# First router of a Macaron block: transposed logits in four column groups, row copies moved behind the PSUM copies, and a quarter of the one-hot tiles on GpSimd

## The chip, the cores and the metric

The kernel runs on one core of one Trainium2 chip. The metric is the device time of one execution in microseconds. Before the change three runs gave a median of 1010.13 us (1009.66 to 1010.32).

## The reference, cut to what matters

The block is a mixture-of-experts feed-forward layer at half weight, attention, and the same feed-forward layer again; each has a layer norm in front. The change lies in the first feed-forward layer's router. There are 4 x 1024 tokens of 128 features, 8 experts with a capacity of 1280 slots each, and two experts per token.

```python
xt = x.reshape(n, D)                      # after the layer norm
logits = xt @ gate_w                      # n x 8
top_logits, top_idx = jax.lax.top_k(logits, k)
router_probs = softmax over the two chosen
exp_rank = cumsum(one_hot(top_idx)) - 1   # place of each token in its expert, first choices ahead
exp_mask = exp_mask * (exp_rank < cap)
exp_batches = einsum('nec,nd->ecd', sec_mask, xt)   # the rows of each expert
...
x = x + 0.5 * _L0_ffn_ref(_layernorm(x), ...)
```

## The kernel before, in words

The work runs in three stages, one code block per engine in each: the first feed-forward layer (from about 0 to 250 us), attention with the second router woven into it, and the second feed-forward layer. The engines' instruction streams are written out by hand and meet through semaphores; within an engine the order of the code is the order of execution. There is no planner.

The change touches only the first part of the first stage, the router. Its work, with the lines of the profile:

- **SyncE (SP)** loads x in four batches of 1024 tokens into `xin` (L758), loads the first two experts' weights (L764 to L766), stores the normalised rows `xrow` to the table `xn_rows` as each batch is ready (L772), clears parts of `bucket` (L778) and later stores expert outputs (L783).
- **TensorE (PE)** forms the centred gate once (L1153, `centre` times `gate`), turns each batch of x with eight transposes (`turn1`, L1116) into two PSUM banks, and forms the logits (`logits1`, L1125): for each tile of 128 tokens the turned x (128 x 128) is the stationary operand and the centred gate (128 x 8) the moving one, so that tokens come out on partitions. The order is turn 0, turn 1, logits 0, turn 2, logits 1, turn 3, logits 2, logits 3. Then come the rank sums of each half of the tokens (`ranks1`, L1133 to L1137), the turns of the attention weights (L1166, L1167), and the two halves of the slot table (`table`, L1147): for each of 16 token tiles and both choices a one-hot tile `b_one` (stationary) meets `a_tok` (moving).
- **ScalarE (ACT)** copies the gate (L1073), copies each turned half batch from PSUM to `xT` (`turned1`, L1070), and normalises the rows (`norm1`, L1062, eight instructions per batch); `norm1(b - 1)` stands behind `turned1(b)`. Then it scales `a_one` by the tile number (`numbers`, L1083), and later runs the experts' gelu (L1102).
- **VectorE (DVE)** clears and sets up constants, takes the row statistics (`stats`, L873 to L882), and then does the routing for each half c of the tokens (a half is 16 tiles, two batches): `choose(c)` (L912 to L928: copy the logits, two rounds of maximum, one-hot and expert number), `rank(c)` (L935 to L949), `one_hots(c)` (`a_one` L953, `a_tok` L957, then 32 tiles of `b_one`, L961, two per token tile). The order is choose 0, choose 1, rank 0, one_hots 0, rank 1, one_hots 1. Behind it stand the copies of the attention weights (L977, L978), and the combination of the table into `slot_tok` (L985 to L989).
- **GpSimd (POOL)** makes iotas and masks, computes each batch's reciprocal deviation (L808, L810), further masks (L811 to L827) and selection tiles (L834), and then waits for `slot_tok` and for `xn_rows`. From there it gathers the experts' rows (L845, 10 gathers per expert, 80 in all) which PE turns (L1177), multiplies (L1186, L1196) and so on.

The four-tile rhythm of the table is `B_STEP = 4`: DVE counts `b_hot` up once after `a_tok` and once after every fourth token tile, and PE waits for it ahead of every fourth tile, and for ACT's `a_num` ahead of each.

Of the kernel before, what the change touches and what calls it, by code (L numbers as in the profile page):

```python
# [5 lines left out]
def macaron_block_kernel(nc, x, wq, bq, wk, bk, wv, bv, wo, bo, gate_w, c_fc, fc_bias, c_proj, proj_bias, out):  # L6
# [17 lines left out]
    P = 128  # L24
    B, S, D = x.shape
    N = B * S
    E, _, F = c_fc.shape
# [128 lines left out]
    with whole:  # L156
# [295 lines left out]
        def experts(tag, dest, gy, ws, bs, rows_ld, w_ld):  # L452
# [237 lines left out]
        SLOTS = E * CT  # L690
        W = TOPK * E
        s_w, s_gate, s_zero = (sem(n) for n in ("s_w", "s_gate", "s_zero"))
        s_iota, s_const, s_cdve, s_wt = (sem(n) for n in ("s_iota", "s_const", "s_cdve", "s_wt"))
# [8 lines left out]
        bucket_zero, xn_st = sem("bucket_zero"), sem("xn_st")  # L702
        gate_mm, gate_ok, s_edge = sem("gate_mm"), sem("gate_ok"), sem("s_edge")
        s_sel = sem("s_sel")
        tr_full, tr_evac, up_full, up_done, dn_full, dn_done, bias_ok = (
            sem(n) for n in ("tr_full", "tr_evac", "up_full", "up_done", "dn_full", "dn_done", "bias_ok"))
        with ExitStack() as part:  # L707
# [19 lines left out]
            high_f = sb1("high_f", [P, U, TOPK])  # L727
            low_f = sb1("low_f", [P, U, TOPK])
            high_b = sb1("high_b", [P, U, TOPK], bf16)
            centre = sb1("centre", [P, P])  # L730
            gate_c = sb1("gate_c", [P, E])
            iota_low = sb1("iota_low", [P, P], bf16)
# [19 lines left out]
            def x_bank(b, half):  # L752
                return bank[2 * (b % 2) + half]

            @block.sync
# [36 lines left out]
            def _(pool):  # L792
# [12 lines left out]
                for b in range(B):  # L805
# [6 lines left out]
                                        pattern=[[0, HS], [-1, P]], channel_multiplier=1).then_inc(s_const, 1)  # L812

                for k, s in enumerate((slice(0, 64), slice(64, 128))):
                    nc.gpsimd.affine_select(out=q_edge[s], in_=q_edge[s], compare_op=ALU.is_ge, fill=NEG, base=STEP * EDGE,
                                            pattern=[[1, P]], channel_multiplier=-STEP).then_inc(s_edge, 1)
                    nc.gpsimd.affine_select(out=k_edge[s], in_=k_edge[s], compare_op=ALU.is_ge, fill=0.0, base=STEP * EDGE,
                                            pattern=[[1, P]], channel_multiplier=-STEP).then_inc(s_edge, 1)
                    pool.wait_ge(s_edge, 5 * k + 2)
                    nc.gpsimd.affine_select(out=k_edge[s], in_=k_edge[s], compare_op=ALU.is_ge, fill=0.0,  # L820
                                            base=STEP - 1 - STEP * EDGE, pattern=[[-1, P]],
                                            channel_multiplier=STEP).then_inc(s_edge, 1)
                    pool.wait_ge(s_edge, 5 * k + 3)
                    nc.gpsimd.affine_select(out=k_edge[s], in_=k_edge[s], compare_op=ALU.is_ge, fill=1.0, base=-EDGE,
                                            pattern=[[0, P]], channel_multiplier=1).then_inc(s_edge, 1)
                    pool.wait_ge(s_edge, 5 * k + 4)
                    nc.gpsimd.affine_select(out=k_edge[s], in_=k_edge[s], compare_op=ALU.is_ge, fill=0.0, base=-KS,  # L827
                                            pattern=[[0, P]], channel_multiplier=1).then_inc(s_edge, 1)
                    pool.wait_ge(s_edge, 5 * k + 5)
                of_head = identb[0:HS * DH, 0:HS * DH].rearrange("p (i s d) -> p i s d", s=2, d=DH)  # L830
                for which, order in enumerate((Q_PART, K_PART)):
                    for c, j in enumerate(order):
                        to = sel[:, which, j].rearrange("p i (s m) -> p i s m", s=2)[:, :, :, c * DH:(c + 1) * DH]
                        nc.gpsimd.tensor_copy(to, of_head).then_inc(s_sel, 1)  # L834
                pool.wait_ge(s_sel, 2 * len(Q_PART))
                pool.wait_ge(slot_ok, 1)
                pool.wait_ge(xn_st, 16 * B)
# [15 lines left out]
            @block.vector  # L853
            def _(dve):
                nc.vector.memset(ident[:], 0.0)
                nc.vector.memset(identb[:], 0.0)
# [52 lines left out]
                def choose(c):  # L909
                    ts = slice(c * U, c * U + U)  # L910
                    dve.wait_ge(lg_full, 2 * c + 2)
                    i = nc.vector.tensor_copy(lgs[:].rearrange("p t e -> p (t e)"), lg_bank[c][:, 0:U * E])  # L912
                    i.then_inc(lg_done, 1)
# [16 lines left out]
                def rank(c):  # L930
# [15 lines left out]
                    step(nc.vector.tensor_scalar(high_i[:], pos_i[:], 7, None, ALU.logical_shift_right))  # L946
                    nc.vector.tensor_copy(low_f[:], low_i[:])
                    step(nc.vector.tensor_copy(high_f[:], high_i[:]))
# [3 lines left out]
                def one_hots(c):  # L952
# [5 lines left out]
                                            ALU.mult).then_inc(b_hot, 1)  # L958
                    for t in range(U):
                        for k in range(TOPK):  # L960
                            i = nc.vector.tensor_scalar(b_one[c][:, t, k, :], iota_low[:], low_f[:, t, k:k + 1], None,  # L961
                                                        ALU.is_equal)
                        if t % B_STEP == B_STEP - 1:
                            i.then_inc(b_hot, 1)
# [83 lines left out]
            def _(act):  # L1048
# [17 lines left out]
                def turned1(b):  # L1066
                    wait(act, lg_full, b - 1)
                    for half in range(2):
                        act.wait_ge(xt_full, 2 * b + half + 1)
                        nc.scalar.copy(xT1[b % 2][:, half * 512:half * 512 + 512], x_bank(b, half)).then_inc(xt_evac, 1)  # L1070

                act.wait_ge(gate_mm, 1)
                nc.scalar.copy(gate_c[:], bank[6][:, 424:424 + E]).then_inc(gate_ok, 1)  # L1073
                turned1(0)
                for b in range(1, B):
                    turned1(b)
                    norm1(b - 1)
                norm1(B - 1)

# [27 lines left out]
            def _(pe):  # L1107
# [11 lines left out]
                def logits1(b):  # L1119
                    if b == 0:  # L1120
                        pe.wait_ge(gate_ok, 2)
                    pe.wait_ge(xt_evac, 2 * b + 2)
                    for t in range(T):
                        c = (b % 2 * T + t) * E
                        i = nc.tensor.matmul(lg_bank[b // 2][:, c:c + E], xT1[b % 2][:, t * P:(t + 1) * P], gate_c[:], start=True,  # L1125
                                             stop=True)
                    i.then_inc(lg_full, 1)
# [13 lines left out]
                def table(c):  # L1141
                    for t in range(U):
                        if t % B_STEP == 0:
                            pe.wait_ge(b_hot, (U // B_STEP + 1) * c + t // B_STEP + 2)
                        pe.wait_ge(a_num, c * U + t + 1)
                        for k in range(TOPK):
# [5 lines left out]
                pe.wait_ge(gate_ok, 1)  # L1152
                nc.tensor.matmul(bank[6][:, 424:424 + E], centre[:], gate[:], start=True, stop=True).then_inc(gate_mm, 1)  # L1153
                turn1(0)
                turn1(1)
                logits1(0)
                turn1(2)
                logits1(1)
                turn1(3)
                logits1(2)  # L1160
                logits1(3)
                ranks1(0)
                ranks1(1)
# [1259 lines left out]
```

## Time and profile before

| what | value |
|---|---|
| median of 3 runs | 1010.13 us |
| profiled execution, its time | 1008.24 us |
| its span | 1006.3 us |
| mean granted TensorE clock | 0.914 |
| PE busy | 818.1 us (81%) |
| DVE busy | 598.4 us (59%) |
| ACT busy | 522.7 us (52%) |
| POOL busy | 489.5 us (49%) |

The span is the profiled execution from its first to its last instruction; 1.9 us of its time lie around it. Busy shares are means over the three stages and say little about the router, which takes the first 57 us. Times within the trace count from the start of the span.

### The profile page before, as it was taken

Reading aid. Unit: us, or ns where it says so; the run is one execution under the profiler, and the core shown is the slowest. Engines: PE = TensorE matmul, PEld = TensorE weight load, DVE = VectorE, ACT = ScalarE, POOL = GpSimd, SP = SyncE. Lnnn points to the kernel's source line nnn. Section 1 sums busy time; section 2 is a strip of 40 time slices with the busy share of each in tenths; the row PEclk is TensorE's granted clock in tenths of the full one; section 3 lists DMA queues with packets and bytes.
Section 4 is the critical chain, followed back from the end, with each engine's and each line's share of the span. In section 5 each row is a group of like instructions: output and inputs, shape, how many; then the busy total and the mean of one; then the engine's idle time right before and its main releaser. Section 6 shows DMA issues by size and latency. Waiting matters only on the chain. (4 is left out here: it accounts for less than half of the span.)

```text
span 1006.3 us, 18072 instructions
## 1 busy us (share of the span) xinstructions
PE 818.1 (81%) x6599; PEld 444.1 (44%) x6599; DVE 598.4 (59%) x1237; ACT 522.7 (52%) x841; POOL 489.5 (49%) x686
## 2 busy tenths in 40 slices
PE   7469999963878888988879888888888509999990
PEld 7447877841323223332323323333133307787780
DVE  7941211223788878888877887868684423234335
ACT  6323243342347767678666786656677204334330
POOL 6047455415655552656468341662225642555453
PEclk9979999995669999999999999989799659999995
DMA  7215576531544161441623505242102125423236
GB/s 197 88 27 156 146 204 170 150 112 38 150 140 141 32 193 37 136 123 26 195 66 103 154 19 159 76 140 61 22 18 89 55 62 173 115 81 101 74 141 233
DMA packets 96184, 110.80 MB, mean 110 GB/s; under 512 B 12279, under 2 KB 68763, under 8 KB 96104
## 3 DMA queue, kind: packets, MB, share of 16 engines
q1 hardware_dynamic: 84968, 89.25, 29.9%
q0 software_dynamic: 9216, 17.98, 6.9%
q10 hardware_dynamic: 1920, 2.51, 0.7%
q8 instruction: 49, 0.80, 0.3%
q14 instruction: 31, 0.25, 0.1%
HBM read 57.86 MB, written 52.89 MB: 110 GB/s over the span
## 5 line engine op out<-in xcount | busy, mean ns | idle before, releaser
L1909 DVE TENSOR_REDUCE m_blk<-banks 128x8 f32<-128x1024 f32 (+1 forms) x320 | 349.5, 1113 | 62.8 <-PE banks L1507 51.0
L1830 ACT ACTIVATE pt<-banks 128x1024 f32<-128x1024 f32 (+3 forms) x384 | 300.7, 812 | 122.2 <-PE banks L1491 118.8
L1539 PE MATMUL banks<-pt,vs 128*32 128x512 f32 (+3 forms) x1536 | 170.8, 518 | 2.6 <-ACT o_sb L1770 2.4
L1491 PE MATMUL banks<-qb,kp 64*128 64x512 bf16 (+3 forms) x768 | 129.2, 342 | 44.2 <-DVE m_blk L1909 40.1
L2265 POOL TENSOR_SCALAR_AFFINE_SELECT pt<-pt 128x512 f32<-128x512 f32 x128 | 81.5, 637 | 167.3 <-ACT pt L1830 167.2
L1507 PE MATMUL banks<-kp,qa 64*128 64x128 bf16 (+4 forms) x1152 | 123.4, 288 | 20.0 <-ACT pt L1830 10.5
L845 POOL DMA_INDIRECT xe<-xn_rows,slot_tok x80 | 79.9, 999 | 91.4 <-PE banks L1186 34.4
L671 POOL DMA_INDIRECT y_tab<-ys,ids x70 | 68.0, 971 | 80.8 <-DVE ys L631 63.8
L1102 ACT ACTIVATE he<-banks,b_up 128x512 f32<-128x512 f32 (+1 forms) x96 | 57.9, 616 | 86.8 <-PE banks L1186 86.5
L1507 PEld LDWEIGHTS banks<-kp,qa 48*128 48x128 bf16 (+1 forms) x1152 | 45.0, 97 | 130.5 <-ACT pt L1830 94.7
L581 ACT ACTIVATE hT<-banks,bfc 128x512 f32<-128x512 f32 (+1 forms) x96 | 56.2, 615 | 84.6 <-DVE bfc L603 48.5
L1491 PEld LDWEIGHTS banks<-qb,kp 64*128 64x128 bf16 x768 | 35.9, 95 | 122.1 <-DVE m_blk L1909 83.2
L1186 PE MATMUL banks<-xeT,w_up 128*128 128x512 f32 (+1 forms) x192 | 73.8, 534 | 2.3 <-DVE xeT L1014 2.3
L1196 PEld LDWEIGHTS banks<-w_dn,he 128*128 128x128 f32 x640 | 73.9, 192 | 3.8 <-issue 3.8
L1196 PE MATMUL banks<-w_dn,he 128*128 128x128 f32 x640 | 75.2, 275 | 0.0
L628 DVE TENSOR_TENSOR ys<-banks,early_b 128x512 f32<-128x512 f32 (+1 forms) x24 | 14.5, 603 | 87.7 <-PE banks L539 87.7
L1023 DVE TENSOR_TENSOR ye<-banks,b_dn 128x512 f32<-128x512 f32 (+1 forms) x24 | 14.5, 603 | 83.1 <-PE banks L1196 83.1
L400 POOL DMA_INDIRECT bucket<-rows,row_ix x48 | 47.8, 996 | 14.5 <-issue 13.6
L1539 PEld LDWEIGHTS banks<-pt,vs 128*32 128x32 f32 x1536 | 30.8, 109 | 47.1 <-issue 32.1
L2278 POOL DMA_INDIRECT gy<-y_slots,y_row x32 | 32.5, 1016 | 36.2 <-POOLq L707 26.8
L1186 PEld LDWEIGHTS banks<-xeT,w_up 128*128 128x128 f32 x192 | 36.2, 196 | 28.1 <-issue 22.7
L1014 DVE COPY xeT<-banks 128x512 f32<-128x512 f32 (+1 forms) x24 | 14.4, 598 | 43.7 <-PE banks L1177 43.7
(339 smaller groups left out, 1127.4 us busy)
## 6 DMA issues: line engine op xcount, KB each, us to landing
bucket<-zero SPq DMA_DIRECT2D x16, 660.0 KB, 5.6
qb<-q_stack SPq DMA_DIRECT2D x32, 192.0 KB, 3.3
qa<-q_stack SPq DMA_DIRECT2D x30, 192.0 KB, 3.8
kp<-k_stack SPq DMA_DIRECT2D x30, 192.0 KB, 4.4
q_stack<-qp SPq DMA_DIRECT2D x18, 256.0 KB
k_stack<-kq SPq DMA_DIRECT2D x18, 256.0 KB
y_slots<-ye SPq DMA_DIRECT2D x16, 256.0 KB, 2.5
mid<-x SPq DMA_DIRECT2D x8, 512.0 KB, 3.4
```

Of the source, the lines that this page charges most:

```text
L581: nc.scalar.activation(hT[par][:, b, 0:n * P], h_bank[b][:, 0:n * P], ACT.Gelu, bias=bfc[q][:, b:b + 1]).then_inc(h_done, 1)
L671: nc.gpsimd.indirect_dma_start(table[:, :], bass.IndirectOffsetOnAxis(ap=ids[q][:, t:t + 1], axis=0), ys[q][:, t, :], None, bounds_check=r ...
L845: nc.gpsimd.indirect_dma_start(xe[q][:, t, :], None, xn_rows[:, :], bass.IndirectOffsetOnAxis(ap=slot_tok[:, e * CT + t:e * CT + t + 1], a ...
L1102: nc.scalar.activation(he[par][:, b, 0:n * P], h_bank[b][:, 0:n * P], ACT.Gelu, bias=b_up[q][:, b:b + 1]).then_inc(up_done, 1)
L1186: nc.tensor.matmul(h_bank[b][:, 0:n * P], w_up[q][:, b * P:(b + 1) * P], xeT[q][:, t0 * P:(t0 + n) * P], start=True, stop=True).then_inc(u ...
L1196: i = nc.tensor.matmul(y_bank[par][:, t * P:(t + 1) * P], he[par][:, b, t * P:(t + 1) * P], w_dn[q][:, b, :], start=b == 0, stop=b == FB - 1)
L1491: i = nc.tensor.matmul(ring[SLOT["score", 2 * u + pair]][:, s, 0:w], kp[g][rows_s, pair, kb * P:(kb + 1) * P], qb[par][rows_s, pair, q0:q0 ...
L1507: i = nc.tensor.matmul(ring[slot][:, s, at:at + blocks * P], qa[par][rows_s, pair, qt * P:(qt + 1) * P], kp[g][rows_s, pair, kb * P:(kb + ...
L1539: i = nc.tensor.matmul(o_bank[VW * h:VW * h + VW, q:q + w], vs[par][:, kb, h, :], pt[u % PTS][:, h, 0:w], start=u in (0, SECOND), stop=u i ...
L1830: nc.scalar.activation(pt[u % PTS][:, 2 * pair:2 * pair + 2, 0:w], ring[SLOT["score", 2 * u + pair]][:, :, 0:w], ACT.Exp, scale=SCALE).the ...
L1909: nc.vector.tensor_reduce(dst, ring[slot][:, :, 0:blocks * P].rearrange("p s (j k) -> p s j k", k=P), AX.X, ALU.max).then_inc(m_done, 1)
L2265: nc.gpsimd.affine_select(out=v, in_=v, compare_op=ALU.is_ge, fill=0.0, base=0, pattern=[[0, HS], [1, P]], channel_multiplier=-1).then_inc ...
```

## The change

- The logits come out transposed: the centred gate, widened with zeros from 8 to 32 columns (`GW`), is the stationary operand, and the turned x of one tile (128 columns) the moving one. The result of tile t stands on 32 PSUM partitions, those of column group t mod 4. ACT copies the result of a batch (128 x 256) to the new tile `lgt`, and PE turns it back with two transposes (`by_token1`), 32 columns per token tile in the logits' bank. `choose` copies 8 of each 32 columns.
- ACT no longer puts a batch of row normalisations between the copies: all four `norm1` stand behind the last copy.
- Of each four token tiles the last one's `b_one` tiles (t = 3, 7, 11, 15 of each half) are made by GpSimd (`last_of_four`), after `a_eq`, with a semaphore `p_hot` on which PE waits ahead of those tiles. `low_f` has two buffers. DVE counts `b_hot` up after the third tile of each four.
- DVE clears the wide gate tile first of all; PE's first matmul and each logits matmul count up `lt_full` in place of `gate_mm` and `lg_full`.

```diff
+        GW = 32
-            gate_c = sb1("gate_c", [P, E])
+            gate_c = sb1("gate_c", [P, GW])
+            lgt = sb1("lgt", [P, 2, 2 * P])
-            low_f = sb1("low_f", [P, U, TOPK])
+            low_f = [sb1(f"low_f{i}", [P, U, TOPK]) for i in range(2)]
+            def lt_bank(b):
+                return bank[4][:, b % 2 * 2 * P:(b % 2 + 1) * 2 * P]
...
+                def last_of_four(c):
+                    pool.wait_ge(a_eq, c + 1)
+                    for t in range(B_STEP - 1, U, B_STEP):
+                        for k in range(TOPK):
+                            i = nc.gpsimd.tensor_scalar(b_one[c][:, t, k, :], iota_low[:], low_f[c][:, t, k:k + 1], None,
+                                                        ALU.is_equal)
+                        i.then_inc(p_hot, 1)
...
                 pool.wait_ge(s_sel, 2 * len(Q_PART))
+                last_of_four(0)
+                last_of_four(1)
                 pool.wait_ge(slot_ok, 1)
...
+                nc.vector.memset(gate_c[:], 0.0).then_inc(lt_evac, 1)
                 nc.vector.memset(ident[:], 0.0)
...
-                    i = nc.vector.tensor_copy(lgs[:].rearrange("p t e -> p (t e)"), lg_bank[c][:, 0:U * E])
+                    i = nc.vector.tensor_copy(lgs[:], lg_bank[c].rearrange("p (t w) -> p t w", w=GW)[:, :, 0:E])
...
                     for t in range(U):
+                        if t % B_STEP == B_STEP - 1:
+                            continue
...
-                        if t % B_STEP == B_STEP - 1:
+                        if t % B_STEP == B_STEP - 2:
                             i.then_inc(b_hot, 1)
...
                 def turned1(b):
-                    wait(act, lg_full, b - 1)
+                    wait(act, lt_full, b if b > 1 else 0)
...
+                def turned_back(b):
+                    act.wait_ge(lt_full, b + 2)
+                    nc.scalar.copy(lgt[:, b % 2, :], lt_bank(b)).then_inc(lt_evac, 1)
...
                 turned1(0)
-                for b in range(1, B):
-                    turned1(b)
-                    norm1(b - 1)
-                norm1(B - 1)
+                turned1(1)
+                turned_back(0)
+                turned1(2)
+                turned_back(1)
+                turned1(3)
+                turned_back(2)
+                turned_back(3)
+                for b in range(B):
+                    norm1(b)
...
+                    wait(pe, lt_evac, b if b > 1 else 0)
                     for t in range(T):
-                        c = (b % 2 * T + t) * E
-                        i = nc.tensor.matmul(lg_bank[b // 2][:, c:c + E], xT1[b % 2][:, t * P:(t + 1) * P], gate_c[:], start=True,
-                                             stop=True)
+                        half, j = divmod(t, 4)
+                        i = nc.tensor.matmul(lt_bank(b)[j * GW:(j + 1) * GW, half * P:(half + 1) * P], gate_c[:],
+                                             xT1[b % 2][:, t * P:(t + 1) * P], start=True, stop=True)
+                    i.then_inc(lt_full, 1)
+
+                def by_token1(b):
+                    pe.wait_ge(lt_evac, b + 2)
+                    for half in range(2):
+                        c = (b % 2 * 2 + half) * P
+                        i = nc.tensor.transpose(lg_bank[b // 2][:, c:c + P], lgt[:, b % 2, half * P:(half + 1) * P], ident[:])
                     i.then_inc(lg_full, 1)
...
+                        if t % B_STEP == B_STEP - 1:
+                            pe.wait_ge(p_hot, (U // B_STEP) * c + t // B_STEP + 1)
...
                 turn1(0)
                 turn1(1)
                 logits1(0)
                 turn1(2)
+                by_token1(0)
                 logits1(1)
                 turn1(3)
+                by_token1(1)
                 logits1(2)
+                by_token1(2)
                 logits1(3)
+                by_token1(3)
                 ranks1(0)
```

## Rows read from the trace of the kernel before

**Rows 1.** Engines by stretch: us, busy (x count) per engine, PEclk, DMA share, GB/s
```profile
0.00:26.50 26.50, 21.23 (x100) 20.67 (x101) 17.94 (x113) 18.16 (x42) 15.42 (x43) 1.00 0.72 200
26.50:57.00 30.50, 15.65 (x133) 12.41 (x131) 29.30 (x121) 7.88 (x35) 0.00 (x0) 1.00 0.17 62
57.00:69.00 12.00, 5.19 (x14) 3.33 (x14) 3.11 (x15) 2.96 (x5) 8.61 (x9) 0.57 0.17 39
```

**Rows 2.** Timeline, 16 to 31 us: start, us, engine, line, op [idle before <-releaser]
```profile
16.53 0.17 DVE L882 TENSOR_SCALAR var<-mv 128x8 f32<-128x8 f32 x1
...
18.07 0.29 DVE L912 COPY lgs<-banks 128x128 f32<-128x128 f32 x1 [1.37 <-PE banks L1125]
...
19.62 6.83 PE L1125 MATMUL banks<-gate_c,xT 128*128 128x8 f32 x32
...
26.49 0.29 DVE L912 COPY lgs<-banks 128x128 f32<-128x128 f32 x1 [3.95 <-PE banks L1125]
...
30.36 0.16 DVE L935 TENSOR_TENSOR taken<-taken,banks 128x16 f32<-128x16 f32 x1
```

**Rows 3.** Timeline, 48 to 58 us, the table's second half and its end
```profile
48.63 5.29 DVE L961 TENSOR_SCALAR b_one<-iota_low,low_f 128x128 bf16<-128x128 bf16 x32
...
50.07 5.00 PE L1147 MATMUL banks<-a_tok,b_one 128*128 128x160 bf16 x32 [6.58 <-DVE b_one L961]
...
53.97 0.91 PEld L1147 LDWEIGHTS banks<-a_tok,b_one 128*128 128x128 bf16 x8 [0.37 <-DVE b_one L961]
...
55.30 0.33 DVE L985 COPY t_sec<-banks 128x160 f32<-128x160 f32 x1
...
57.95 1.26 POOL L845 DMA_INDIRECT xe<-xn_rows,slot_tok  x1 [32.94 <-DVE slot_tok L989]
```

**Rows 4.** Timeline of PE: transposes and matmuls in the router, among the experts, in attention
```profile
7.83 1.97 PE L1116 MATMUL banks<-ident,xin 128*128 128x128 f32 x8 [0.32 <-DMA xin<-in_L_attn_x_dram]
...
62.43 0.66 PE L1177 MATMUL banks<-ident,xe 128*128 128x128 f32 x2 [7.36 <-DMA xe<-xn_rows,slot_tok]
...
63.87 3.75 PE L1186 MATMUL banks<-xeT,w_up 128*128 128x256 f32 x8 [0.78 <-DVE xeT L1014]
...
86.27 1.89 PE L1186 MATMUL banks<-xeT,w_up 128*128 128x256 f32 x8
...
410.18 0.43 PE L1539 MATMUL banks<-pt,vs 128*32 128x128 f32 x8
```

**Rows 5.** Loads of x: last two issues; issue to landing of all four, of the third
```profile
1.93 3.69 SPq L758 DMA_DIRECT2D xin<-in_L_attn_x_dram  x2
...
DMA to landing us min/median/max: 4.7/7.4/9.5
...
DMA to landing us min/median/max: 8.2/8.2/8.2
```

**Rows 6.** Timeline of ACT: copies and row normalisations
```profile
19.86 0.59 ACT L1070 COPY xT<-banks 128x512 f32<-128x512 f32 x1 [0.21 <-PE banks L1116]
...
20.35 6.26 ACT L1062 ACTIVATE xrow<-xin,sh,rs 128x128 f32<-128x128 f32 x16
```

**Rows 7.** Timeline: DVE and POOL at work together
```profile
2.95 1.16 DVE L865 MEMSET zero<- 128x1320 f32 x1 [0.22 <-issue]
...
3.20 1.13 POOL L803 TENSOR_SCALAR_AFFINE_SELECT before<-before 128x128 bf16<-128x128 bf16 x1
...
18.64 0.63 POOL L811 TENSOR_SCALAR_AFFINE_SELECT causal<-causal 128x512 bf16<-128x512 bf16 x1
18.72 0.70 DVE L918 TENSOR_TENSOR eqs<-lgs,top 128x128 f32<-128x128 f32 x1
...
19.46 0.29 DVE L920 TENSOR_TENSOR cands<-eqs,place 128x128 f32<-128x128 f32 x1
19.54 0.36 POOL L817 TENSOR_SCALAR_AFFINE_SELECT k_edge<-k_edge 64x128 bf16<-64x128 bf16 x1
```

**Rows 8.** Groups of POOL by form: count, busy us, mean ns
```profile
L2239 POOL TENSOR_SCALAR m_neg<-m_of 128x16 f32<-128x16 f32 x32 | 8.3, 260 | 34.2 <-DVE m_of L1914 34.1
```

More of the change, by code:

```diff
@@ L702, in macaron_block_kernel @@
         bucket_zero, xn_st = sem("bucket_zero"), sem("xn_st")
-        gate_mm, gate_ok, s_edge = sem("gate_mm"), sem("gate_ok"), sem("s_edge")
+        gate_ok, s_edge = sem("gate_ok"), sem("s_edge")
         s_sel = sem("s_sel")
+        lt_full, lt_evac, p_hot = (sem(n) for n in ("lt_full", "lt_evac", "p_hot"))
         tr_full, tr_evac, up_full, up_done, dn_full, dn_done, bias_ok = (
@@ L946, in rank @@
                     step(nc.vector.tensor_scalar(high_i[:], pos_i[:], 7, None, ALU.logical_shift_right))
-                    nc.vector.tensor_copy(low_f[:], low_i[:])
+                    nc.vector.tensor_copy(low_f[c][:], low_i[:])
                     step(nc.vector.tensor_copy(high_f[:], high_i[:]))
@@ L959, in one_hots @@
                     for t in range(U):
+                        if t % B_STEP == B_STEP - 1:
+                            continue
                         for k in range(TOPK):
-                            i = nc.vector.tensor_scalar(b_one[c][:, t, k, :], iota_low[:], low_f[:, t, k:k + 1], None,
+                            i = nc.vector.tensor_scalar(b_one[c][:, t, k, :], iota_low[:], low_f[c][:, t, k:k + 1], None,
                                                         ALU.is_equal)
-                        if t % B_STEP == B_STEP - 1:
+                        if t % B_STEP == B_STEP - 2:
                             i.then_inc(b_hot, 1)
@@ L1070, in turned1 @@
                         nc.scalar.copy(xT1[b % 2][:, half * 512:half * 512 + 512], x_bank(b, half)).then_inc(xt_evac, 1)
-                act.wait_ge(gate_mm, 1)
-                nc.scalar.copy(gate_c[:], bank[6][:, 424:424 + E]).then_inc(gate_ok, 1)
-                turned1(0)
-                for b in range(1, B):
-                    turned1(b)
-                    norm1(b - 1)
-                norm1(B - 1)
+                def turned_back(b):
+                    act.wait_ge(lt_full, b + 2)
+                    nc.scalar.copy(lgt[:, b % 2, :], lt_bank(b)).then_inc(lt_evac, 1)
+                act.wait_ge(lt_full, 1)
+                act.wait_ge(lt_evac, 1)
+                nc.scalar.copy(gate_c[:, 0:E], bank[6][:, 424:424 + E]).then_inc(gate_ok, 1)
+                turned1(0)
+                turned1(1)
[7 more added lines that the diff above has]
+                    norm1(b)
                 def numbers(c):
@@ L1152, in _ @@
                 pe.wait_ge(gate_ok, 1)
-                nc.tensor.matmul(bank[6][:, 424:424 + E], centre[:], gate[:], start=True, stop=True).then_inc(gate_mm, 1)
+                nc.tensor.matmul(bank[6][:, 424:424 + E], centre[:], gate[:], start=True, stop=True).then_inc(lt_full, 1)
                 turn1(0)
```

## The prediction

> **What bounds the kernel now.** I read the stretches first, then the timeline at each boundary. The router is the first 57 us. Up to 26.5 us PE is the busiest engine, with 21.2 us; from there to 57 us DVE is, with 29.3 of 30.5 us, while POOL does nothing at all [rows 1]. The hand-over shows in the waits ahead of the first instruction of each `choose`: DVE idles 1.37 us for the logits of the first half, though its statistics end at 16.70, and 3.95 us for those of the second, which end at 26.45 [rows 2]. From 26.49 on DVE runs on to the table: `choose(1)` takes 3.87 us, up to the `taken` at 30.36 [rows 2], and ranks and one-hots fill the rest. The table's last matmul ends at 55.07, 0.23 us before DVE, which has come through its weight copies, reads it at 55.30; POOL's first gather follows at 57.95, and POOL had stood 32.94 us for it [rows 3]. All later work hangs on the gathers. So two things set the 57 us: when the second half of the logits is there, and how long DVE works behind it.
>
> A caution on the clock. The column says 1.00 up to 57 us [rows 1], but eight transposes take 1.97 us there, 0.22 us from one to the next and a tail of 0.2. At 62.43, in a stretch with a mean of 0.57, two take 0.66, which is the same rate [rows 1, 4]. I price PE's router work at that rate, that of the 1.2 GHz level. What the 2.4 GHz level is worth is seen in the two rows of 256-column matmuls, 3.75 and 1.89 us: a factor of two [rows 4].
>
> **The logits.** Removed: 64 records of 6.83/32 = 0.214 us, 3.42 us per batch [rows 2]. Added per batch: 16 records with 32 stationary and 128 moving columns in four column groups. The nearest row is attention's, 8 such records in 0.43 us at the high level, of which about 0.2 is tail [rows 4]. That leaves 0.21 for eight; doubled for the count and again for the clock it is 0.85 us, and the tail. Were the groups not to overlap at all, it would be four times that, 3.4 us, as before. I take 0.85, since that row has this form. Further per batch: two transposes, 0.44 us and the tail [rows 4]; and a copy of 128 x 256 on ACT, which I put at 0.45 from 0.59 for 512 columns [rows 6].
>
> Now the order, with each start. The third batch of x is issued at 1.93 and lands 8.2 us later, at 10.1; the fourth takes 9.5 us from an issue that ends at 5.62 and starts, for a length of 1.8, near 3.8: 13.3 [rows 5]. Turn 1 is issued until 9.6; logits 0 to 10.45; turn 2 to 12.2; back-turn 0 to 12.7 (its ACT copy is done at 11.2); logits 1 to 13.5; turn 3 to 15.3; back-turn 1 to 15.7, done at 16.0. Logits 2 to 16.6; then PE waits for its own result to come back through ACT (tail 0.25, copy 0.45, a semaphore each way), and back-turn 2 is issued from 17.4 to 17.8; logits 3 to 18.7, the same round trip, back-turn 3 done at about 20.2. The second half of the logits is there 6.2 us before 26.45.
>
> **DVE then.** `choose(0)` is no longer held by PE but by the statistics, whose end at 16.70 stays [rows 2]. Alone it takes 3.87 us as `choose(1)` does, and POOL's masks add 0.5 (0.41 of it to `eqs` [rows 7]): 16.75 to 21.1. `choose(1)` then starts at once, its logits having been there for 0.9 us, and ends at 25.2, with 0.2 us for those masks that now fall in it and no longer in DVE's pause. The rank sums are no hindrance: PE does those of the first half between the two. `rank(0)` starts at 25.2 instead of 30.36: **5.2 us gained**. What is late next is DVE itself.
>
> The strided copy of the logits has 128 elements as before: nothing. The memset of the wide gate adds up to 0.1 us to DVE's first work and to PE's first matmul, but the first x lands at 0.79 + 4.7 = 5.5 [rows 5], and PE has 1 us to spare before it: nothing.
>
> **ACT's order.** The 32 normalisations, 6.26/16 = 0.39 us each [rows 6], start at 19.7 and end at 32.2, not 26.6. SP's last store of rows, and behind it on its queue the two clears of `bucket`, are issued 5.6 us later. The gathers that read the rows began 31 us after the last normalisation (57.95 less 26.6); 19 us are left of that, so it costs nothing. `numbers(0)` finds `a_one` ready at about 30.9 and starts 1.3 us late; it feeds the first half of the table alone, which PE has done by 37.5, while the second begins past 43. If that cover failed it would cost 1.3 us at most.
>
> **The one-hots.** 16 of 64 tiles leave DVE, at 5.29/32 = 0.165 us each [rows 3]: 2.64 us less, half of it in each `one_hots`, both on the path. POOL shows no such operation at 128 columns. Below stands a `TENSOR_SCALAR` of 16 columns, 0.26 [rows 8], beside it a mask of 128 columns, 0.36, above it one of 512 with 0.63 [rows 7]. I take 0.35, as the columns are the same; 8 tiles are 2.8 us, in which DVE makes its 24 in 4.0, so POOL is not late. Behind POOL's waits for `a_eq` stand only the gathers, which wait longer still. The price is another: POOL and DVE get in each other's way. A POOL mask of 128 columns took 1.13 us and ended 0.2 us after DVE's 1.16 us memset; and DVE's `eqs`, whose like takes 0.29, took 0.70 while POOL was at `causal`, 0.41 lost to 512 columns [rows 7]. In proportion a tile of 128 costs DVE 0.11 us; the bounds are nothing and a whole tile. DVE's stream has no gaps, so I take 0.11 for each of the 16, 1.8 us: net **0.9 us gained**.
>
> The Trainium skill ("SBUF — State Buffer", section "Who interferes with whom") has it that the ports shared by the two are an exclusive lock, kept by whichever came first for its whole instruction. The mask behind the memset agrees; the `eqs` row lost less than `causal` took. By that rule a tile would cost its 0.35 us, 5.6 in all, and the sum would be 2.2 us.
>
> PE's table is next in line. A group of four tiles takes 1.10 us to its end (53.97 to 55.07) and came every 1.30 us [rows 3]; now one can come every 0.99 to 1.2. So the last ends at most 0.2 us after DVE is ready for it; with the 1.8 us above DVE is the later one, and I put nothing.
>
> **Sum.** 5.2 + 0.9 = 6.1 us. The profiled execution, 1008.24 us (span 1006.3), would become 1002.1; it lay 1.9 us below the median of the runs, and against this median I predict **1004.0 us**. A measurement of this kernel tells about 0.2%, or 2.0 us, from no change.
>
> **Rivals.**
> *POOL's tiles cost DVE nothing.* Short instructions may slip between each other: `cands` kept its 0.29 us while POOL was at `k_edge` [rows 7]. Then 5.2 + 2.64, less 0.15 for the table: 7.7 us, 1002.4. Chance 0.17.
> *A tile costs DVE its whole time.* For it the mask behind the memset, against it `eqs` and `cands`. With 0.29 to 0.35 us, 4.6 to 5.6 of 7.8 us come back: 1006.9 to 1007.9. Chance 0.16. (This is what the page above would give.)
> *The same, and slower than before.* The balance tips at 7.84/16 = 0.49 us of DVE's time per tile. If the comparison costs POOL as much as the 512-column mask, 0.63, then 10.1 - 7.8 = 2.3 us are lost: 1012.4. The 0.26 of the 16-column row speaks against it. Chance 0.03.
> *The column groups do not overlap.* Place: PE ahead of `choose(1)`. Each batch costs 3.42 + 0.45 us, and the last two back-turns add two round trips of 0.7: the logits are there at about 30.2, 3.7 us late, and less 0.9 for the tiles this gives 1012.9. It turns slower once a batch's logits cost over some 2.6 us. The attention row speaks clearly against it. Chance 0.03.
> *Part is lost at the hand-over to the experts.* PE meets its gathered rows at the low level and leaves it some us later. If the rise does not move with the work but comes one step late, eight matmuls behind it run at half rate; by the difference of the 256-column rows, 1.9 us [rows 4], that is up to 1.9: 1005.9. Attention can add the same with either sign. Chance 0.11.
>
> **The numbers.** The forecast has 0.50. The range takes in the first, second and fifth rival: 1001.4 to 1008.0; 1 us under the cheapest sum is for clock steps later on. Faster by over 0.2% is under 1008.1: 0.91. Within 0.2%: 0.04, the upper edge of the second rival with the fifth. Slower: 0.05, nearly all of it from the two rivals at 1012.
>
> **What would show it.** Right, if the 16 logits records of a batch take 1.0 to 1.2 us; if `choose(0)` starts at 16.7 with no wait for PE and `choose(1)` directly behind it; if `rank(0)` starts near 25.2; if ACT's normalisations end near 32; if DVE's 24 `b_one` take about 4.8 us and not 4.0, with POOL's eight tiles inside; and if the first gather is issued at 51.8. Wrong, if DVE waits for PE ahead of `choose(1)`, if the `b_one` stretch is over 5.3 us, or if the gather comes 6 us earlier and the end does not.

## The result, and the profile after

| | before | after |
|---|---|---|
| median | 1009.94 us (20 runs) | 1004.45 us (20 runs) |
| profiled execution, its span | 1008.24, 1006.3 us | 1002.15, 1000.4 us |
| PE, DVE busy | 818.1, 598.4 us | 805.3, 596.0 us |
| first gather issued (trace) | 57.95 us | 49.86 us |

The ratio is 0.9943 with a 95% interval of 0.9915 to 0.997: 5.8 us less, between 3.0 and 8.6. The forecast was 1004.0 us and 6.1 us less. The ratio leaves out one run of the changed kernel, 1013.57 us, that counts as slow; medians and means have it in. Single executions of either kernel spread over some 15 us, of which more below.

The same stretches as in [rows 1], now divided at 20.5 us, behind the logits (us; busy and count of PE, PEld, DVE, ACT, POOL; PEclk; DMA share; GB/s):

```profile
0.00:20.50 20.50, 10.57 (x109) 7.99 (x110) 17.75 (x115) 10.91 (x24) 11.86 (x26) 0.96 0.69 182
20.50:49.90 29.40, 14.19 (x132) 12.60 (x130) 28.02 (x106) 16.42 (x57) 15.73 (x35) 0.62 0.36 118
```

DVE is now the busiest of the engines in both. PE's work up to the logits has halved, in part because it ran at its high level from 8.8 to 19.0 us: the eight transposes of the third batch take 1.10 us here and took 1.95 before. The timeline that answers to [rows 2], 5 to 25 us of the changed kernel:

```profile
5.08 1.65 DVE L890 BATCH_NORM_STATS2 st<-xin 128x6 f32<-128x128 f32 x8 [0.85 <-DMA xin<-in_L_attn_x_dram]
...
9.05 0.64 PE L1155 MATMUL banks<-xT,gate_c 128*32 128x128 f32 x16
...
15.75 0.65 PE L1155 MATMUL banks<-xT,gate_c 128*32 128x128 f32 x16
...
16.08 0.16 DVE L899 TENSOR_SCALAR var<-mv 128x8 f32<-128x8 f32 x1
16.15 0.28 DVE L929 COPY lgs<-banks 128x128 f32<-128x128 f32 x1
...
16.73 12.42 ACT L1081 ACTIVATE xrow<-xin,sh,rs 128x128 f32<-128x128 f32 x32
...
16.89 0.44 PE L1163 MATMUL banks<-ident,lgt 128*128 128x128 f32 x2 [0.49 <-ACT lgt L1093]
...
20.02 0.28 DVE L929 COPY lgs<-banks 128x128 f32<-128x128 f32 x1
...
24.05 0.16 DVE L952 TENSOR_TENSOR taken<-taken,banks 128x16 f32<-128x16 f32 x1
```

Neither `choose` waits for PE any more: both copies (L929) come without an idle time in front. The last turn back is done at 17.33, 2.7 us before DVE wants it; `rank(0)` starts at 24.05 instead of 30.36, 6.3 us earlier. Of these 0.45 belong to no part of the change: in this execution the first x landed at 5.08 instead of 5.53. In the fourteen traces of this case it lands anywhere from 4.96 to 5.53, with either router, and the statistics follow it without a gap.

The one-hots and the table's end, to be held against [rows 3]:

```profile
40.65 0.89 DVE L974 TENSOR_SCALAR a_tok<-a_one,pid 128x2560 bf16<-128x2560 bf16 x1
40.71 6.09 POOL L824 TENSOR_SCALAR b_one<-iota_low,low_f 128x128 bf16<-128x128 bf16 x8 [4.88 <-DVE a_one L970]
41.45 4.27 DVE L980 TENSOR_SCALAR b_one<-iota_low,low_f 128x128 bf16<-128x128 bf16 x24
...
46.85 0.11 PEld L1186 LDWEIGHTS banks<-a_tok,b_one 128*128 128x128 bf16 x2 [0.32 <-POOL b_one L824]
...
47.27 0.33 DVE L1004 COPY t_sec<-banks 128x160 f32<-128x160 f32 x1 [0.17 <-PE banks L1186]
...
49.86 1.29 POOL L861 DMA_INDIRECT xe<-xn_rows,slot_tok  x1 [3.06 <-DVE slot_tok L1008]
```

DVE's stretch is 4.27 us instead of 5.29. POOL's eight tiles take 6.09 us and end at 46.80, after DVE's; PE waits 0.32 us for the last of them, and DVE waits 0.17 us for PE. From `rank(0)` to `t_sec` it is 23.22 us, where it was 24.94: 1.7 us gained. So the router is 8.1 us shorter in this trace, 7.6 without the earlier load, and the span only 5.9.

### The profile page after: what moved, and what is told of

Read it like the earlier page. It is cut to its first block and busy times, and to the rows that moved or that the text cites. A ratio compares the mean times of both kernels' runs of the same rounds, so it can differ in the third digit from the quotient of the medians.

```text
span 1000.4 us, 18105 instructions
## 1 busy us (share of the span) xinstructions
PE 805.3 (80%) x6607; PEld 431.0 (43%) x6607; DVE 596.0 (60%) x1222; ACT 524.4 (52%) x845; POOL 503.3 (50%) x702
## 5 line engine op out<-in xcount | busy, mean ns | idle before, releaser
L1033 DVE COPY xeT<-banks 128x512 f32<-128x512 f32 (+1 forms) x24 | 14.3, 597 | 43.8 <-PE banks L1220 43.8
```

## The experiments

A mean is that of all timed runs of a kernel, with its standard error. For the changed kernel 32 runs (20 and the 12 below) give 1004.7 ± 0.7 us, for the kernel before 107 runs 1010.5 ± 0.3. A ratio is to the kernel before, with its 95% interval. "High level" and "low level" are TensorE at 2.4 and at 1.2 GHz.

### The changed kernel again

> The changed kernel once more. Theory A (the router's gain arrives whole at the end): the first gather is issued near 50 us instead of 58, and the ratio to the kernel before is that gain over 1010, 0.992. Theory B (part of it is lost behind the router, at the steps of TensorE's clock): the first gather is as early, but the end gains 5 to 6 us only, ratio 0.994 to 0.995, and the difference between the two traces shrinks at a place where the granted clock rises later relative to the work. TensorE's rate in the first 20 us: if the high level there belongs to the change, 16 logits records take 0.64 us again; if it is chance, some run shows about 1.1 us.

Median 1004.42, ratio 0.9943 (0.9916 to 0.997). First gather 49.8. The high level came at 11.6 us instead of 8.8 after the start; so the first batch of logits took 1.08 us, at the low level, and the others 0.64. The router repeats to 0.1 us all the same, while the span was 996.8, 3.6 us less than in the first trace: with the new logits, what varies lies behind the router.

### Without GpSimd's tiles

```diff
-                last_of_four(0)
-                last_of_four(1)
...
-                        if t % B_STEP == B_STEP - 1:
-                            continue
```

> The change without GpSimd's tiles: DVE makes all 64 one-hot tiles. By the trace of the changed kernel the tiles are worth 1.7 to 2.0 us, so the first gather is issued 1.7 to 2.0 us later than in the changed kernel (near 51.8), the ratio is about 0.994 to 0.996. By my forecast (0.11 us of DVE's time per tile) they are worth 0.9 us: gather near 50.8. A rival: they are worth nothing, because GpSimd ends last and the table waits for it: gather near 50.

First gather at 51.61, 1.75 us later than with them: the expected 1.7 to 2.0 holds, and the 0.9 of the prediction was too little. Ratio 0.9959 (0.9934 to 0.9984).

### GpSimd's tiles alone, on the kernel before

```diff
+                last_of_four(0)
+                last_of_four(1)
```

(with the skipped tiles, waits and the second `low_f` of the change)

> The kernel before with nothing but GpSimd's tiles. Theory: 1.7 to 2.0 us earlier at the first gather than the kernel before (57.95 less 1.9, near 56.1), a ratio of 0.998. Rival (DVE loses a whole tile's time, 0.7 us, for each): the gather comes 8 us later, ratio 1.008. Each GpSimd tile should take 0.6 to 0.7 us as in the changed kernel.

First gather at 56.0, 1.9 us earlier, of which 0.14 are an earlier load of x; POOL's stretches 5.88 and 6.08 us, DVE's 4.28 and 4.27 as in the change. Ratio 0.9981 (0.9951 to 1.001), which by itself is not told from no change. The tiles are worth the same with either logits: 1.75 us on top of the new ones, 1.8 on the old.

### Each GpSimd tile by itself

```diff
+                    dve.wait_ge(p_hot, (U // B_STEP) * (c + 1))
                     for t in range(U):
```

> The change with DVE held back: its b_one tiles of each half wait until GpSimd's eight are done, so that GpSimd works with DVE at rest (but for DVE's a_tok ahead). Theory: a GpSimd tile costs about 0.6 us by itself, the seven behind the first show 0.6 us each and DVE's presence added little; my forecast had put it at 0.35. Rival: 0.35 by itself and doubled by DVE: the tiles then show 0.3 to 0.4. DVE's 24 tiles should show the bare 0.165 each, 4.05 us a stretch instead of 4.28.

One run gave 1014.5 us, with the first gather at 58.4. Tiles of the half (timeline, first half) and, by form, DVE's:

```profile
29.90 5.29 POOL L824 TENSOR_SCALAR b_one<-iota_low,low_f 128x128 bf16<-128x128 bf16 x8 [5.25 <-DVE a_one L970]
```
```profile
L981 DVE TENSOR_SCALAR b_one<-iota_low,low_f 128x128 bf16<-128x128 bf16 x48 | 8.0, 247 | 9.2 <-POOL b_one L824 9.2
```

A tile costs POOL 0.60 us (median) with DVE at rest and 0.71 beside it. The first of each half takes 1.2 to 1.3 us in both runs, for DVE's `a_tok` of 0.89 is under way. DVE's 48 tiles take 8.0 us; with POOL at work they took 8.6. So DVE's tiles lost 0.6 us to POOL's 16, 0.035 each, and POOL's lost 0.6 us in the first half (5.89 less 5.29) and 0.74 in the second. The theory holds: the cost of POOL to DVE is a third of what the prediction had taken, that of POOL's own work 1.7 times.

### The order of ACT put back

```diff
                 turned_back(0)
+                norm1(0)
                 turned1(2)
                 turned_back(1)
+                norm1(1)
...
```

> The change with ACT's normalisations put back between the copies, in the order of before. If they have to stand behind (each batch holds the next copies up by 3.2 us), the fourth logits are ready near 24 instead of 17.3 us and choose of the second half waits: worked out from the rows, the copies of batches 2 and 3 go from 10.6 and 13.8 to about 13.8 and 17.5, the last turn back to 22 or 23, rank(0) starts near 27 instead of 24.05, and the first gather is 2.5 to 3 us later than in the changed kernel. Rival: DVE is the bound and has 2.7 us to spare for the logits of the second half, so it costs under 1 us.

```profile
18.26 0.38 ACT L1093 COPY lgt<-banks 128x256 f32<-128x256 f32 x1
18.52 3.21 ACT L1081 ACTIVATE xrow<-xin,sh,rs 128x128 f32<-128x128 f32 x8
21.61 0.37 ACT L1093 COPY lgt<-banks 128x256 f32<-128x256 f32 x1
```
```profile
22.76 0.29 DVE L929 COPY lgs<-banks 128x128 f32<-128x128 f32 x1 [2.78 <-PE banks L1165]
```

The last batch's transposed logits, done on PE at 20.2, lie until ACT has done eight normalisations; DVE waits 2.78 us. (About 0.25 of it is that PE, idle for so long, did the last turn back at the low level, 0.69 us instead of 0.44.) First gather 52.5, 2.7 later than in the change; ratio 0.9986 (0.9956 to 1.0015). The new order is worth 2.7 us, but only with the new logits, as the next run shows.

### The order alone, on the kernel before

```diff
                 for b in range(1, B):
                     turned1(b)
-                    norm1(b - 1)
-                norm1(B - 1)
+                for b in range(B):
+                    norm1(b)
```

> The kernel before with nothing but the order of ACT changed: the four batches of normalisations behind the last copy, logits as before. PE was the bound there and waited for no copy longer than 0.5 us, so theory: the logits of the second half end at 26.3 to 26.5 and the first gather stays near 58. Rival: the order alone gives part of the gain, the logits end one or more us earlier. A cost to look for: ACT's numbers(0) start later than a_one, since the normalisations end near 32.

The logits end at 26.05 and the first gather comes at 57.5, where x had landed 0.4 us earlier: nothing gained, as expected. 1011.3 us in one run.

### Column groups: neighbours, and one group against four

```diff
-                    for t in range(T):
+                    for t in (0, 4, 1, 5, 2, 6, 3, 7):
```

> The change with the logits matmuls of a batch in the order 0, 4, 1, 5, 2, 6, 3, 7, so that two neighbours share a column group. If the four groups work at the same time, the order costs: of 16 records at the high level only neighbours of different groups overlap, five steps of 0.21 us and a tail, 1.2 to 1.3 us instead of 0.64. Rival: the rate is set by the issue of the instructions or the 32-column loads, whatever the group: 0.64 again. The first gather does not move in either case, as DVE starts choose(0) at the end of its own statistics.

0.66 us per batch at the high level instead of 0.64: I was wrong, the order within the batch costs 0.02 us and not 0.6. Was it the groups at all?

```diff
+                for t in range(T):
+                    half = t // 4
+                    nc.tensor.matmul(rk_bank[0][0:GW, half * P:(half + 1) * P], gate_c[:], xT1[1][:, t * P:(t + 1) * P], start=True,
+                                     stop=True)
+                for t in range(T):
+                    half, j = divmod(t, 4)
+                    nc.tensor.matmul(rk_bank[0][j * GW:(j + 1) * GW, half * P:(half + 1) * P], gate_c[:],
+                                     xT1[1][:, t * P:(t + 1) * P], start=True, stop=True)
```

(16 matmuls more, first eight all in the first group, then eight spread over the four; each of them stands as two records)

> The change with two blocks of eight more logits matmuls in PE's pause behind the last turn back (results not used): first all eight in column group 0, then in four groups as the change has them. If the groups are what makes them fast, the first block takes four times as long per record (16 records, 1.7 us at the high level) as the second (0.44 and a tail of 0.2). Rival: a 128-column record costs the same whatever the group, 0.64 us for either block, and the gain came from loading 32 instead of 128 columns. The first gather stays at 50, the blocks end before the rank sums at 20.

```profile
17.08 1.83 PE L1207 MATMUL banks<-xT,gate_c 128*32 128x128 f32 x15
18.64 0.31 PE L1211 MATMUL banks<-xT,gate_c 128*32 128x128 f32 x3
18.74 0.27 PE L1207 MATMUL banks<-xT,gate_c 128*32 128x128 f32 x1
18.77 0.68 PE L1211 MATMUL banks<-xT,gate_c 128*32 128x128 f32 x13
```

In one group (L1207) 15 records take 1.83 us with the tail, and start 0.109 us apart; in four (L1211) all 16 are through in 0.81, the first of them still behind the block before. In the undisturbed batches of 0.64 us it is four records every 0.109 us, 0.027 each. Both blocks load the same 32 columns, so the rival that the narrow load made the gain is out: the groups make the difference, fourfold but for the tail, and the order of the tiles in the batch does not.

### The kernel before against itself, and a delay

> The kernel before against itself. Both theories of the loss behind the router expect a ratio of 1.000 and a router as before (first gather near 57.5 to 58, by the landing of x). If the place of a kernel in a round counted, the ratio would be off here too. From first gather to the last ye the traces so far fall into two lots, 159.6 to 161.3 us and 162.6 to 163.1; the kernel before was in the first. If chance decides, it may be in either now.

Ratio 0.9981 (0.9949 to 1.0013): no difference, as it must be. But the router of this execution was another one:

```profile
7.49 1.75 PE L1116 MATMUL banks<-ident,xin 128*128 128x128 f32 x8 [0.30 <-DMA xin<-in_L_attn_x_dram]
9.07 1.85 PE L1125 MATMUL banks<-gate_c,xT 128*128 128x8 f32 x16
10.78 1.07 PE L1116 MATMUL banks<-ident,xin 128*128 128x128 f32 x8
11.69 2.87 PE L1125 MATMUL banks<-gate_c,xT 128*128 128x8 f32 x16
14.41 1.95 PE L1116 MATMUL banks<-ident,xin 128*128 128x128 f32 x8
16.15 6.83 PE L1125 MATMUL banks<-gate_c,xT 128*128 128x8 f32 x32
```
```profile
9.00:12.00 3.00, 3.00 (x31) 3.00 (x28) 2.90 (x31) 2.94 (x8) 2.37 (x3) 1.00 1.11 285
12.00:26.50 14.50, 13.24 (x86) 12.97 (x85) 10.83 (x57) 12.22 (x31) 9.48 (x29) 0.51 0.67 203
```

The same 16 records take 1.85, 2.87 and 3.42 us: TensorE was at the high level from 9 to 12 us and at the low one after. PE is the bound there, so the first gather came at 54.50, 3.45 us earlier than in the trace of before (0.33 of it by the load). In two more traces with the old logits (the order alone, GpSimd's tiles alone) all four batches took 3.42. So one trace in four with the old logits shows a high level in the router, for some 3 us; of the ten with the new logits every one does, from between 8.7 and 11.6 us on. Whether the change brings this about was not tested.

```diff
                 dve.wait_ge(table_full, 2)
+                for _ in range(3):
+                    step(nc.vector.tensor_tensor(idle_out[:], a_one[1][:], a_one[1][:], ALU.mult))
```

> The change with three products of 2560 columns on DVE (2.8 us each, 8.5 us together, result not used) between the end of the table and its copy, so that the router ends as late as that of before, about 58.4 us at the first gather. Theory 1 (a router's microsecond is a microsecond at the end, all else is chance): mean of the runs 1004.7 + 8.5 = 1013.2 us. Theory 2 (some 2 to 3 us of an earlier router are lost behind it because of when the later work comes): the time is that of the kernel before plus 0.5, 1010 to 1011 us.

The three products took 4.54 us and not 8.5, so that the first gather was issued at 54.44, 4.6 us later than in the changed kernel. The mean is 1009.6 ± 0.9, ratio 0.9979 (0.995 to 1.0007): 4.9 ± 1.1 us above that kernel's mean, so within the noise a microsecond at the router is one at the end. The prices named for the two theories were made for 8.5 us and cannot be used; by the delay there was, theory 1 expects 1009.3. Theory 2 expects 1006.3 to 1007.3 if the whole 2 to 3 us are swallowed, two to three standard errors too low, but 1007.7 to 1008.2 if they are swallowed in proportion, which this run does not exclude. The traces say where such a loss would have to be: not at the hand-over, for from the first gather to the last `ye` (the first layer's last expert output) it is 161.5 ± 0.7 us in the four with the old logits and 161.6 ± 0.5 in the ten with the new. Behind it the means are 791.0 ± 1.4 and 791.9 ± 1.0, too wide to tell a loss of 2 us from none. Theory 2 is not needed for any measurement here, but it is not excluded.

### A busy TensorE between table and experts

```diff
+                keep(8)
                 pe.wait_ge(slot_ok, 1)
+                keep(12)
                 transposes(0, 0, 0, 0)
```

(`keep(n)` issues n bf16 matmuls of 512 columns whose result nobody uses; `slot_ok` is DVE's signal that `slot_tok` is there)

> The change with 8 idle matmuls (512 columns, bf16, result not used) behind the table and 12 behind slot_tok, so that TensorE does not rest between the table and the first gathered rows. Theory (a varying part is lost at the hand-over, because the low level lasts to 5 or to 13 us after PE meets the gathered rows): at the high level from the start, the first expert's first chunk takes 1.9 instead of 3.75 us, and the time from first gather to the last ye is 158 to 160 us, where it was 159.6 in two traces, 161.3, 162.6 and 162.8 in others; ratio 0.990 to 0.994. Rival: the gathers set the pace there and the loss is elsewhere: ratio as the changed kernel, 0.994. If PE is at the low level when they start, they run into the first transposes and cost up to 2.5 us.

```profile
48.00:54.50 6.50, 4.28 (x20) 1.63 (x18) 3.88 (x17) 0.00 (x0) 3.29 (x3) 0.99 0.08 20
55.00:68.00 13.00, 10.41 (x20) 5.64 (x20) 1.19 (x3) 4.33 (x7) 6.53 (x7) 0.50 0.17 39
```

The twenty ran at the high level and ended at 52.3; after 2.3 us of rest two transposes (0.44 us) still ran at it, then it fell before the first expert matmuls and stayed low for 13 us. So TensorE did rest before the gathered rows, and the run does not show what an unbroken stream would do. From the first gather to the last `ye` it was 163.1 us. Mean 1008.1 ± 1.1, ratio 0.9968 (0.9939 to 0.9997): no gain over the change, probably a loss.

### DVE relieved further

```diff
-                nc.vector.memset(rows_l[:, :, D:ROW], 0.0)
...
-                    nc.vector.tensor_copy(w[:], bank[4][:, n * P:(n + 1) * P])
+                    nc.scalar.copy(w[:], bank[4][:, n * P:(n + 1) * P])
...
-                    for t in range(B_STEP - 1, U, B_STEP):
+                    for t in range(B_STEP - 1, U - B_STEP * c, B_STEP):
```

(that memset and eight more small instructions go behind the `y_row` work; ACT's copies stand between `numbers(0)` and `numbers(1)`; DVE makes the very last token tile, and PE waits for it with a semaphore of its own)

> The change, and DVE relieved on the router's path: constants that only attention needs are set in DVE's pause behind y_row, the copies of the attention weights go to ACT between numbers(0) and numbers(1), and DVE instead of GpSimd makes the very last token tile of the table. If DVE is the bound from the statistics to slot_tok, choose(0) starts 0.3 to 0.4 us earlier, GpSimd is no longer last at the table, and the first gather is issued 0.7 to 0.9 us earlier, near 49.1. Rival: the landing of x or the table holds it, under 0.3 us. The ratio, 0.993 to 0.994, cannot tell this apart, only the trace can.

```profile
5.45 1.65 DVE L890 BATCH_NORM_STATS2 st<-xin 128x6 f32<-128x128 f32 x8 [1.22 <-DMA xin<-in_L_attn_x_dram]
...
16.20 0.28 DVE L920 COPY lgs<-banks 128x128 f32<-128x128 f32 x1
...
40.73 4.73 POOL L824 TENSOR_SCALAR b_one<-iota_low,low_f 128x128 bf16<-128x128 bf16 x6 [4.87 <-DVE a_one L961]
41.47 4.61 DVE L971 TENSOR_SCALAR b_one<-iota_low,low_f 128x128 bf16<-128x128 bf16 x26
...
46.66 0.32 DVE L993 COPY t_sec<-banks 128x160 f32<-128x160 f32 x1
```

First gather 49.25, 0.6 us earlier; `t_sec` waits for nobody. `choose(0)` started at 16.20 where it was 16.15, but in this execution x landed at 5.45 instead of 5.08. Counted from the landing, `choose(0)` is 0.3 us earlier (10.75 instead of 11.07 us behind it) and the first gather 1.0 (43.8 instead of 44.8): 0.3 from the set-up moved away and 0.65 from the table's end, and the later load hid the 0.3. The mean of 6 runs is 1003.1 ± 0.9, ratio 0.9908 (0.9876 to 0.9941). It beats the kernel before; that it beats the change is shown by the trace alone, as 1.6 ± 1.1 us between the means is too little.

## Why the prediction was right

The mechanisms were right, but that the time came out 0.45 us from the forecast is partly luck: two terms were too small, by 0.7 and 0.8 us, and most of what they gave more is missing again in the means of the runs.

**The logits, 5.2 us.** Right in its steps: `choose(0)` at the end of the statistics, `choose(1)` behind it without a wait, logits ready in time. Measured 6.3, less 0.45 for the load, 5.9. Of the 0.7 more, 0.5 is that `choose(0)` took 3.87 us flat, where the prediction had booked 0.5 us for POOL's masks: `causal` (18.19 to 18.88) this time met a product, a reduction and the head of `eqs`, and none of them took over 0.30 us. A batch of logits took 0.64 and not 1.0 to 1.2 us, since PE was at the high level; the one that ran at the low level took 1.08, as priced. It changed nothing, as DVE was the bound. With the low level throughout, the forecast had the last logits ready at 20.2, and DVE asked for them at 20.0; no trace shows that case. The rival of groups that do not overlap is refuted by the run with one group against four.

**ACT's order.** The cover was right: nothing waited for the normalisations, which ended at 29.2 and not 32.2, since with PE at the high level they began 3 us sooner. The prediction named no price for the order. It is worth 2.7 us, inside the 5.9 of the logits and only with them.

**The one-hots, 0.9 us.** The term that was mis-sized is the 0.11 us of DVE per tile: it measured 0.035, and the part is worth 1.75 to 1.8 us. (A quarter of the 0.41 us lost to 512 columns is 0.10, too; that slip is 0.1 us in the sum.) The other price in it, 0.35 us per POOL tile, was 0.60 alone and 0.71 beside DVE. Because POOL needs 6.1 us, it is POOL and PE's table that end last, by 0.17 us, where the prediction had DVE. The first rival, no cost to DVE, was the nearer one: its sum was 7.7 us, and DVE's tiles lost 0.6 us to 16 of POOL's. The Trainium skill ("SBUF — State Buffer", section "Who interferes with whom") has the other engine wait for a whole instruction. If each of POOL's 16 tiles held DVE up for its measured 0.60 us, DVE would have lost 9.6 us by that rule, an estimate; the 0.6 us measured do not agree with it, or DVE's `b_one` do not need the shared ports, which no run here decides. POOL's first tile of each half does agree: it began behind `a_tok` and took 0.6 and 0.7 us longer than the others alone.

**The sum.** 7.6 us by the pair of traces, and 5.8 ± 0.8 by the means of the runs. What did not hold is a premise of the prediction's first part, that PE's router work runs at the low level: in the one trace there was it did, in the control it did not throughout, and that router was 3.1 us shorter. The kernel before is PE-bound there and inherits PE's level; the changed one is DVE-bound and does not. Counted from the landing of x, the first gather of the old router comes after 52.4 us in three traces (with 1.8 added for the one with GpSimd's tiles) and after 49.3 in one, that of the changed kernel after 44.8 to 44.9 in all five traces that leave its router as it is. So the gain is 6.8 ± 0.8 us on average, against 5.8 ± 0.8 from the means: what is missing, 1.0 ± 1.1, is no more than the noise. The delay shows the passage from router to end to be one for one within ± 0.25. How often the old router is the short one was not counted; how much of the difference is this and how much noise stays open.

**The hand-over.** The fifth rival's mechanism is real, its price was not 1.9 us, and nothing ties it to the change. From the first gather to the last `ye` it took 159.6 or 159.7 us in the traces of before, of the change, of its repetition and of the kernel with DVE relieved further; 161.3 in three (without GpSimd's tiles, the control, one group against four); and 162.6 to 163.1 in the seven others. The first eight records of 512 columns on PE behind the gathers sort the traces the same way: 3.70 us in the first four, 5.40 in the three, 6.2 to 6.7 in the seven. Of the change, and of the kernel with the old order of ACT:

```profile
61.56 3.70 PE L1229 MATMUL banks<-xeT,w_up 128*128 128x512 f32 x8 [0.78 <-DVE xeT L1033]
```
```profile
56.70:70.00 13.30, 10.86 (x21) 5.77 (x22) 1.19 (x3) 4.34 (x7) 6.98 (x7) 0.50 0.19 41
```
```profile
64.67 6.38 PE L1231 MATMUL banks<-xeT,w_up 128*128 128x512 f32 x8 [0.78 <-DVE xeT L1033]
```

In the latter the low level lasted 13 us behind PE's start (56.76), and the eight records took 6.38 us instead of 3.70. In the change it lasted 5.9 us. Both happened with either kind of router. I take it for chance, 3.5 us wide, but with one trace per kernel that is not shown. Behind the last `ye` the spans differ by another 11 us (787.4 to 798.6), with either router; what makes that difference was not looked into.

## What to carry to other kernels

Where an engine's rate has two levels, ask of every stretch whether that engine is its bound: the old router's time changed by 3 us from one execution to the next, the new one's not, and a single trace shows only one of the cases. A reordering can be worth nothing alone and 2.7 us with another change, since it frees only what the other has made late. And work given to an idle engine should be priced by that engine's own row for the operation; here it was 0.60 us per tile instead of the 0.35 taken from other operations, and only because DVE had its weight copies to do behind its own tiles did no more than 0.17 us of it count.

## What the runs showed of the hardware that was not expected

- The clock column reads 1.00 up to 54.8 us in the trace of before, though every matmul there ran at the rate of 1.2 GHz; in the control, where the column reads 0.51 for 12 to 26.5 us, the same records take the same 3.42 us. A 1.00 at the head of a trace is to be checked against durations.
- A GpSimd `TENSOR_SCALAR` of 128 x 128 bf16 with a scalar per partition takes 0.60 us; the mask of the same shape (`identb`) 0.29. DVE loses 0.035 us for each that runs beside its own short ones, GpSimd 0.09 a tile on average (12.0 less 10.6 us for 16).
- 32-column float32 matmuls in four column groups run four times as fast as in one (0.027 against 0.109 us per record at the high level), and the order of the groups within a batch of eight changes 0.64 us to 0.66.
- Twenty idle matmuls that ended 2.3 us before the real ones did not keep TensorE at its high level: the two transposes behind the rest still took 0.44 us, the eight records of 256 columns from 55.8 us on took 3.75, as at the low level.
